# Four cross-attention layers on one core: outputs one tile further behind, output biases as weight rows, 112 columns, other places for the side steps

## What is computed

```
q = x @ wq;  k = ctx @ wk;  v = ctx @ wv             (per head)
out = softmax(q @ k.T * scale) @ v @ wo + bo         (cross-attention, three times)
```

## Time and profile before

| | us |
|---|---|
| median of 3 runs | 6159.2 (6155.66 to 6174.12) |
| the profiled execution | 6158.75 |
| its span, first to last instruction | 6156.9 |
| phase 0, 16 pairs | about 190 to 2850, a pair is about 165 |
| phase 1, 16 pairs | about 2850 to 3840 |
| phase 2, 16 pairs | about 3990 to 6157, a pair is about 136 |

### The profile page before, as it was taken

How to read it: one execution, slowest core, us unless ns; L and a number is a source line. 1 busy time by engine, 2 the same in 40 slices (tenths; PEclk the granted TensorE clock), 3 DMA queues, 4 the chain that set the end, 5 groups by cost and what they waited for, 6 DMA issues and landing times.

```text
span 6156.9 us, 92602 instructions
## 1 busy us (share of the span) xinstructions
PE 5728.1 (93%) x34384; PEld 4613.2 (75%) x34384; DVE 2843.0 (46%) x5170; ACT 3105.5 (50%) x7280; POOL 3112.4 (51%) x3472
## 2 busy tenths in 40 slices
PE   7999999999999999998999998899999999999998
PEld 5777777777777777776666666677777777777776
DVE  2444444444444444443555554344445554444452
ACT  1445554444554444453555454255555555555554
POOL 0444444444444444453555555155556555555564
PEclk9899999999999999997999999599999999999999
DMA  2000000000000000000111011000000000000000
GB/s 55 12 16 16 16 13 15 16 15 16 16 12 13 12 15 16 16 20 17 29 29 29 24 33 37 8 18 15 18 15 20 18 19 15 16 16 17 15 19 10
DMA packets 84429, 114.48 MB, mean 19 GB/s; under 512 B 42814, under 2 KB 64682, under 8 KB 83978
## 3 DMA queue, kind: packets, MB, share of 16 engines
q1 hardware_dynamic: 83978, 108.56, 6.2%
HBM read 104.06 MB, written 4.46 MB: 18 GB/s over the span
## 4 chain that ended last, share of the span: by engine, by line
PE 59%; DVE 13%; issue 11%; POOL 10%; ACT 4%; DMA 3%; POOLq 0%; SPq 0%; DVEq 0%; ACTq 0%
PE ps_c L687 11%; POOL p_lo L1606 9%; PE ps_c L1068 6%; PE ps_u L1141 5%; PE ps_s L1126 4%; PE ps_u L1143 4%; PE ps_u L1142 4%; PE ps_s L1128 4%; PE ps_s L1127 4%; DVE mpiece L1450 4%; PE ps_c L1087 3%; DMA w_area<-recs 1%; DVE uT L1477 1%; PE ps_c L893 1%; PE ps_c L867 1%
## 5 line engine op out<-in xcount | busy, mean ns | idle before, releaser
L1606 POOL TENSOR_TENSOR p_lo<-p,p_hi 125x448 fp32r<-125x448 f32 (+2 forms) x2688 | 2709.9, 1018 | 2257.6 <-ACT p_hi L1819 2163.1
L1817 ACT ACTIVATE p<-ps_s 125x448 f32<-125x448 f32 (+2 forms) x2688 | 1326.8, 494 | 2125.8 <-PE ps_s L1128 2023.6
L1819 ACT ACTIVATE p_hi<-ps_s 125x448 fp32r<-125x448 f32 (+2 forms) x2688 | 1318.6, 491 | 0.0
L1450 DVE TENSOR_REDUCE mpiece<-ps_c 125x1 f32<-125x500 f32 (+1 forms) x1984 | 1235.7, 669 | 123.9 <-PE ps_c L1068 116.8
L1141 PE MATMUL ps_u<-p_hi,ctx_hi 125*97 125x448 f32 (+2 forms) x2688 | 997.3, 371 | 103.2 <-POOL p_lo L1606 93.8
L1126 PE MATMUL ps_s<-q_hi,ctxT_hi 105*125 105x448 f32 (+3 forms) x2688 | 992.7, 369 | 22.6 <-DVE q_hi L1460 17.6
L1068 PE MATMUL ps_c<-ctxT_hi,q_hi 96*125 96x500 f32 (+1 forms) x2112 | 863.8, 431 | 87.7 <-DVE mpiece L1450 70.8
L1127 PE MATMUL ps_s<-q_lo,ctxT_hi 96*125 96x448 f32 (+2 forms) x2688 | 928.5, 345 | 0.0
L1128 PE MATMUL ps_s<-q_hi,ctxT_lo 96*125 96x448 f32 (+2 forms) x2688 | 926.0, 344 | 0.0
L1143 PE MATMUL ps_u<-p_lo,ctx_hi 125*97 125x448 f32 (+2 forms) x2688 | 918.3, 342 | 0.0
L1142 PE MATMUL ps_u<-p_hi,ctx_lo 125*96 125x448 f32 (+2 forms) x2688 | 917.4, 341 | 0.0
(11 more groups left out here) (231 smaller groups left out, 6006.1 us busy)
## 6 DMA issues: line engine op xcount, KB each, us to landing
...
```

Source lines behind the costliest of these rows:

```text
L1450: z = V.tensor_reduce(mpiece[0:wide, k, r:r + 1], C(0, wide, n % banks(t), 0, PIECE), AX.X, ALU.max)
L1606: P.tensor_tensor(p_lo[0:kp, k % 3, 0:w], p32[0:kp, k % 2, 0:w], p_hi[0:kp, k % 3, 0:w].bitcast(F32), ALU.subtract).then_inc(*sig("pl_ready"))
L1817: A(p32[0:kp, k % 2, 0:w], ps_s[0:kp, k % 2, 0:w], ACT.Exp, scale=DH[t.ph] ** -0.5)
L1819: A(p_hi[0:kp, k % 3, 0:w], ps_s[0:kp, k % 2, 0:w], ACT.Exp, scale=DH[t.ph] ** -0.5)\
```

## The change

1. **Outputs three tiles behind.** `BEHIND` = 3, `RING` = 4: `outputs(n-3)` follows `scores(n)`; `p_hi` gets a fourth buffer. `p32` keeps two and `p_lo` three. ACT copies one group of `uT` after each of the tiles 0, 1, 2 (two after tile 0 and one after tile 1 before; in phase 1 the one copy stands after tile 2, not 1).
2. **Biases as weight rows.** `b_out` (both), `bo2`, `o1_b`, `o2_b` are loaded into a row below the weights (`w_n` row 96, `w_s` and `w_o` row 80); `xT` has a row 80 of ones, and row 96 of `uT` is multiplied by its own reciprocal and so becomes 1. Their one-row matmuls are gone, and the matmul that takes the row has 81 or 97 rows. `bo1` and the feed-forward biases stay as they were.
3. **112 columns.** The key projection of phase 0, the scores of the self-attentions of phases 0 and 2 and two copies of keys leave out the unused 8 of 64 slots.
4. **Products apart.** The products of `uT` stand 4 half-tiles apart (15, 19, 23) in phases 0 and 2.
5. **More room.** In `PARTS` some steps of `pre` and the start of `post` get more distance from what they wait for; the first `pre` of the next phase starts 10, not 4, half-tiles after `POST`.
6. To make space `hm32` goes into `w_s`, and `xnF` shares the tile `xn`.

```diff
+RING = 4
+BEHIND = RING - 1
...
-        p_hi = sb("p_hi", [KP, 3, 448], F32R)
+        p_hi = sb("p_hi", [KP, RING, 448], F32R)
...
-            "pre": ((40, 3, {4: 1, 7: 0.5, 8: 3, 10: 1, 14: 1.5, 16: 3, 18: 2, 22: 2, 27: 2, 30: 1, 34: 1, 35: 0.5, 37: 1,
+            "pre": ((40, 3, {4: 1, 7: 0.5, 8: 3, 10: 1.5, 14: 1.5, 16: 3, 18: 2, 22: 2, 27: 2.5, 30: 1.5, 34: 1, 35: 0.5, 37: 1,
...
-            "post": ((15, 3, {6: 1, 14: 1}), (2, 1.5, {}), (15, 3, {6: 1.5})),
+            "post": ((15, 3, {1: 1, 6: 1, 14: 1}), (2, 1.5, {}), (15, 3, {1: 0.5, 6: 1.5})),
...
-                    lanes = [lane([part("pre", side.pre, At(t.ph + 1, 0, ahead=True))], POST + 4.0)]
+                    lanes = [lane([part("pre", side.pre, At(t.ph + 1, 0, ahead=True))], POST + 10.0)]
...
                     r = side_banks(t)(0, 128, bank, 0, D)
-                    mm(r, ones[DC:DC + 1, :], rows[t.ph][:, D * bias:D * bias + D], start=True, stop=False)
-                    both(r, lambda i: xT[:, i, :, :], lambda i: w[:, i, :], first=False).then_inc(*sig("rm_psum"))
+                    both(r, lambda i: xT[0:HF + i, i, :, :], lambda i: w[0:HF + i, i, :]).then_inc(*sig("rm_psum"))
...
-                            z = both(C(0, 128, 0, 128 * j, 128), lambda i: l1_w[w][:, i, 128 * j:128 * j + 128],
-                                     lambda i: hT[:, i, :, :])
+                            each = slice(0, T if w else S)
+                            z = both(C(0, 128, 0, 128 * j, 128).rearrange("p (b s) -> p b s", b=2)[:, :, each],
+                                     lambda i: l1_w[w][:, i, 128 * j:128 * j + 128], lambda i: hT[:, i, :, each])
...
-                    if t.ph != 1:
-                        mm(r, ones[DC:DC + 1, :], rows[t.ph][:, D * (2 - t.ph // 2):D * (3 - t.ph // 2)], start=True, stop=False)
                     for h in range(t.heads):
-                        z = mm(r, uT[0:DC, h, :, :], w_n[:, h, :], start=(t.ph == 1 and h == 0), stop=(h == t.heads - 1))
+                        k = DC + (t.ph != 1 and h == 0)
+                        z = mm(r, uT[0:k, h, :, :], w_n[0:k, h, :], start=(h == 0), stop=(h == t.heads - 1))
...
-                for n in range(total + 2 if last else total):
+                for n in range(total + BEHIND if last else total):
...
-                    if n >= 2 or not first:
-                        outputs(n - 2)
+                    if n >= BEHIND or not first:
+                        outputs(n - BEHIND)
...
-                        yield POST - 1 + g
+                        yield POST - 1 + (1 if t.ph == 1 else 4) * g
...
-                    act.wait_ge(*got("pv_done", t, k - 2))
-                    A(p_hi[0:kp, k % 3, 0:w], ps_s[0:kp, k % 2, 0:w], ACT.Exp, scale=DH[t.ph] ** -0.5)\
+                    act.wait_ge(*got("pv_done", t, k - BEHIND))
+                    A(p_hi[0:kp, k % RING, 0:w], ps_s[0:kp, k % 2, 0:w], ACT.Exp, scale=DH[t.ph] ** -0.5)\
                         .then_inc(*sig("exp_done"))
-                    if n < 2 and not first:
+                    if n < BEHIND and not first and n - BEHIND + len(G) >= 0:
 
                         yield 2 * n + 2
-                        copy_out(b - 1, range(len(G) - 1, len(G)) if n else range(len(G) - 1))
+                        copy_out(b - 1, (n - BEHIND + len(G),))
```

More of the change, by code:

```diff
@@ L1668, in pre @@
                         act.wait_ge(*got("ot_psum", t, 1))
-                        A(xT[:, :, :, :], side_banks(t)(0, HF, 1, 0, 256).rearrange(two, a=2, b=2), ACT.Copy)\
+                        A(xT[0:HF, :, :, :], side_banks(t)(0, HF, 1, 0, 256).rearrange(two, a=2, b=2), ACT.Copy)\
                             .then_inc(*sig("ot_ready"))
@@ L1706, in pre @@
                         act.wait_ge(*got("ot_psum", t, 1))
-                        A(xT[:, :, :, :], side_banks(t)(0, HF, 0, 0, 256).rearrange(two, a=2, b=2), ACT.Copy)\
+                        A(xT[0:HF, :, :, :], side_banks(t)(0, HF, 0, 0, 256).rearrange(two, a=2, b=2), ACT.Copy)\
                             .then_inc(*sig("ot_ready"))
```

84 lines of the change are left out of this document (44 added, 40 removed).

## The result

| | before | after |
|---|---|---|
| median | 6157.9 us of 4 runs (6155.66 to 6174.12) | 7182.76 us of 4 runs (7166.49 to 7196.23) |
| span of the profiled execution | 6156.9 | 7175.8 |
| mean granted clock | 0.958 | 0.875 |

The ratio is 1.1657, with a 95% interval of 1.1624 to 1.1689: **16.6% slower**, where the forecast was 2.9% faster. The profile shows where the time lies. First the page of the changed kernel: busy times (compare), the granted clock in 40 slices, and the chain that ended last, by engine and by line.

What follows compares the result with a forecast made beforehand. TensorE, busy 93%, was taken to bound the kernel, its largest wait being the outputs' for `p_lo`. Terms 104 + 37 + 18 + 25 - 4 = 180 us off 6158.75 gave 5978 us, own range 5925 to 6040, with rivals 5900 to 6065.

Steps and rivals of the forecast that it cites:

- The step that failed: Broadcast and products of `uT` with 97 partitions instead of 96: same elements per partition, so priced at nothing.
- Rival C: `rb` comes a tile later, DVE waits at its first product and PE behind it: slower, 6203 us at 3.5 per half; chance 0.03.
- the third tile: Outputs three behind cover PE's stops for `p_lo` in phases 0, 2 and the last halves: 104 us, bounds 45 and 157.
- I take 0, since the product stands where it stood: Later copy of `uT` ends its chain a tile, about 1.2 us, later; cost taken as 0.
- Rival A: Stops only change their name, scores waiting for exponentials and reductions for DVE; outputs three behind bring 45: 6038 us; chance 0.20.
- Rival D: Covered stops return at the next wait and only removed work counts: about 6150 us, hardly any change; chance 0.04.
- Rival B: With fewer stops, PE's half-clock pieces in phases 0 and 2 could go, 33 us more: 5945 us; chance 0.13.
- Bias rows: 80 one-row matmuls removed over the phases at 0.47 us each: 37 us, bounds 22 and 42.
- Columns: Self-attention scores of phases 0 and 2, 9 us each, the key projection 0: 18 us, bounds 9 and 32.
- Room, products and `POST + 10`: More room for PE's waits for `q_hi`, `kvb` and `pT` gives 25 us; later `pre` at phase ends costs 4.
- The signs: Profile after: `p_lo` wait below 25 us, phase 0 transposes waiting for `sm`, PE busy about 55 us lower, idle about 125.

Runs made afterwards that it cites:

- b_rows97: The kernel before with the broadcast of the reciprocals (`rb`) written to 97 rows instead of 96, the added row unused: 7256.15 us, ratio 1.1788.
- b_behind3: The kernel before with only the outputs three tiles behind, `RING` of 4 and the later copy of `uT`: 6131 us, ratio 0.9952.
- a_memset: The changed kernel with `rb` broadcast to 96 rows again and the ones in `uT` written by a DVE memset: 6037.01 us, ratio 0.9801.

## Why the prediction was wrong

**The step that failed** is one sentence on the bias rows: "The extra work elsewhere (a broadcast and products with 97 partitions instead of 96) has the same elements per partition: nothing." That holds for the product: with 448 columns it took 0.62 us on 97 partitions in the changed kernel and 0.62 on 96 in `b_rows97`, where DVE waits as long. It does not hold for the broadcast, a transfer: with one row more it took 18.5 us instead of 3.3. It was priced at zero; it cost about 1100 us (1097 put into the kernel before, 1143 taken out of the changed one). No row of the trace of before could show 97 rows, and the forecast put no bounds on this step.

**Rival C**, with a chance of 0.03, had the place right: DVE standing at its first product for `rb`, PE behind it at the maxima, slower from 2.8 us per half. The cause it named (a later start, worth 1.2 us) was not the one, and its price of 3.5 us per half became 12.2, so that the rival was right in its place by luck. The later start is real as well: it is a part of what the third tile lost at first, and "I take 0, since the product stands where it stood" was wrong in its own right. DVE's waits at the reciprocal and the product of phases 1 and 2 rose by 51 and 42 us in `b_behind3`, and PE's for `mpiece` by 47.

**Rival A** (stops only change their name) describes a part: the outputs' wait became ACT's wait for `p_lo` and DVE's for the chain of `uT`, PE's idle time stayed as it was, and the third tile alone gave 27 us, even less than its 45. **Rival D** (nothing remains but the work removed) is refuted by `a_memset`. **Rival B** is taken up below.

**The four terms**, from the parts alone. The third tile, 104 (its lower bound of 45 was called a third, which would be 35 of the 104 or 52 of the 157): the rest gave 85, the clock took 54. By phases the rest gave 56 us in phase 0, for which 26 was taken, 44 in phase 2, for which 69 was, and lost 12 in phase 1, for which nothing was. Right in it: the stops for `p_lo` go (93.8 us to 1.0), and the loop through `p32` binds three tiles near 3.4 us. Bias rows, 37: 47 in the rest, since the one-row matmul also delays the step onto it and the projection behind it. Columns, 18: 21 in the rest, the key projection gives nothing, as said. Room, products and `POST + 10`, 21: nothing in the rest and 58 by the clock. That the time of this part came out better than forecast is luck, for the clock was no term of the sum.

**The signs.** In `a_memset`, the change as it was meant, the outputs wait 1.0 us for `p_lo` and the transposes of phase 0 wait for `sm` (14.0 us in 14 stops), both as forecast. But PE's busy time is lower by 100 us, not 55, and its idle time by 8, not 125.

**What the method missed.** The forecast treated the clock as a rival that can only come back (B: "with fewer stops the pieces at half clock could go"). With the third tile there were fewer stops and more half-clock time, 638 against 529 us: many short stops went, and fewer, longer ones came. The rest came to 148 of 180; the medians followed the clock about as much as the rest.
